# First attention with keys on partitions in a second score pass

## The reference

```
q = layernorm((x @ Wq.T) per head); k = layernorm((x @ Wk.T) per head); v = (x @ Wv.T) per head
scores = where(causal, q @ k.T, -1e30)
x = softmax(scores) @ v, heads joined, @ Wo.T + bo
```

## Time and profile before

| what | us |
|---|---|
| runs, lowest / median / highest | 4074.95 / 4082.11 / 4089.76 |
| profiled execution, its own time | 4099.86 |
| its span | 4098.0 |
| TensorE, VectorE, ScalarE busy | 3508.8, 3057.7, 2302.6 |
| GpSimd busy | 805.5 |
| probability transposes, TensorE busy | 730.8 |
| block copies on VectorE / ScalarE | 597.5 / 233.0 |
| accumulator reads on ScalarE | 437.6 |

### The profile page before, as it was taken

The page is one execution under the profiler, slowest core; times in us unless marked ns, Lnnn a source line. Parts: engine busy times, 40 slices in busy tenths (PEclk is TensorE's granted clock), DMA queues, the critical chain, the costliest instruction groups (busy, mean ns, idle before and its releaser), DMA issues.

```text
span 4098.0 us, 93072 instructions
## 1 busy us (share of the span) xinstructions
PE 3508.8 (86%) x31392; PEld 2764.5 (67%) x31392; DVE 3057.7 (75%) x6444; ACT 2302.6 (56%) x6346; POOL 805.5 (20%) x951
## 2 busy tenths in 40 slices
PE   3898888989889898897988989888898888989888
PEld 2676766767667676676766767667676766767667
DVE  3778777687777877778777687877878777787776
ACT  2655546565465654646646466554656546565464
POOL 1212222022220222202222122221212222022220
PEclk9899999999999998999989989999999999999999
DMA  3000000000000000000000000000000000000000
GB/s 73 7 2 7 7 7 7 2 7 7 7 7 2 7 7 7 7 1 12 2 7 7 7 7 2 7 7 7 7 2 7 7 7 7 2 7 7 6 2 6
DMA packets 33906, 30.35 MB, mean 7 GB/s; under 512 B 8864, under 2 KB 33312, under 8 KB 33376
## 3 DMA queue, kind: packets, MB, share of 16 engines
q1 hardware_dynamic: 33376, 23.68, 2.0%
HBM read 15.28 MB, written 8.39 MB: 6 GB/s over the span
## 4 chain that ended last, share of the span: by engine, by line
PE 57%; issue 14%; DVE 12%; ACT 10%; POOL 5%; SPq 1%; ACTq 0%; DVEq 0%; DMA 0%; POOLq 0%
PE bank L625 12%; PE scores L723 9%; ACT prob L839 6%; PE bank L636 6%; PE scores L612 6%; PE bank L735 4%; PE scores L613 4%; PE scores L614 3%; PE bank L596 2%; POOL qf L503 2%; PE scores L697 2%; PE scores L608 2%; PE scores L677 2%; DVE negmax L1055 1%; PE bank L555 1%
## 5 line engine op out<-in xcount | busy, mean ns | idle before, releaser
L839 ACT ACTIVATE prob<-scores,negmax 128x128 f32<-128x128 f32 (+3 forms) x2048 | 1060.7, 538 | 221.8 <-DVE negmax L1055 178.6
L1055 DVE TENSOR_REDUCE negmax<-scores 128x1 f32<-128x128 f32 (+3 forms) x2048 | 885.4, 484 | 101.0 <-PE scores L614 87.6
L625 PE MATMUL bank<-ident,prob 128*128 128x128 f32 x5120 | 730.8, 280 | 44.9 <-DVE probt L1063 35.6
L1063 DVE COPY probt<-bank 128x512 f32<-128x512 f32 x896 | 597.5, 685 | 179.2 <-PE bank L625 172.2
L625 PEld LDWEIGHTS bank<-ident,prob 128*128 128x128 f32 x5120 | 548.2, 142 | 156.0 <-DVE probt L1063 66.3
L614 PE MATMUL scores<-mask,ident 128*128 128x128 bf16 x2048 | 450.0, 231 | 0.0
L612 PE MATMUL scores<-khh,qt 128*128 128x256 f32 (+2 forms) x1024 | 438.4, 429 | 13.3 <-ACT qt L810 7.5
L839 ACT ACTIVATION_READ_ACCUMULATOR prob<-scores,negmax 128x1 f32 x2048 | 437.6, 214 | 0.0
L810 ACT ACTIVATE probt<-bank 128x512 f32<-128x512 f32 x384 | 233.0, 607 | 205.6 <-PE bank L625 205.6
L613 PE MATMUL scores<-kll,qt 128*128 128x256 f32 (+2 forms) x1024 | 345.4, 337 | 0.0
L596 PE MATMUL bank<-ident,stk 128*128 128x128 bf16 x2048 | 203.8, 286 | 153.2 <-DVE stk L1153 122.2
(11 more groups left out here) (179 smaller groups left out, 6967.4 us busy)
## 6 DMA issues: line engine op xcount, KB each, us to landing
x_in<-in_x_rows SPq DMA_DIRECT2D x16, 512.0 KB, 3.5
out_rows<-x SPq DMA_DIRECT2D x16, 512.0 KB, 3.6
r_gu<-in_wg SPq DMA_DIRECT2D x2, 512.0 KB, 5.0
r_gu<-in_wu SPq DMA_DIRECT2D x2, 512.0 KB, 5.5
r_d<-in_wd SPq DMA_DIRECT2D x1, 1024.0 KB, 6.8
r_wqt<-in_wq_nope_t SPq DMA_DIRECT2D x1, 512.0 KB, 6.2
r_wqr<-in_wq SPq DMA_DIRECT2D x2, 256.0 KB, 8.8
r_wob<-in_wo SPq DMA_DIRECT2D x1, 512.0 KB, 5.3
```

The costliest lines, as they stand in the source:

```text
L625: ins = nc.tensor.transpose(bank[4 + n % 2][:, q * P:(q + 1) * P], prob[:, u % 2, q, i * P:(i + 1) * P], ident[:, :])
L839: nc.scalar.activation(prob[:, u % 2, q, 0:n], bank[q][:, 0:n], ACT.Exp, bias=negmax[:, a, u, q:q + 1], accum_out=sums[:, a, u, q:q + 1]). ...
L1055: nc.vector.tensor_reduce(negmax[:, a, u, M * part:M * part + M], scores[:, M * part:M * part + M, 0:n], axis=AX.X, op=ALU.max, negate=Tru ...
L1063: nc.vector.tensor_copy(probt[:, u % 2, i], bank[4 + n % 2][:, :]).then_inc(probt_dve.sem, 1)
```

## The change

The second attention keeps its code (the index for which attention it is goes away). The first attention has an order of its own, `attend_first`:

- **First score pass.** `score_first` computes the scores with queries on partitions in 11 fills per group (`fill`: the four heads of tile 0 share a bank, two heads of tile 1 do, tiles 2 and 3 take a bank each), in a ring of banks 0 to 2. They are used only for the maximum (`max_first`).
- **The maximum as two rows.** VectorE splits a group's 16 columns of negated maxima in two bf16 parts (`split_max`), TensorE transposes them into bank 7, VectorE copies them to `nmt`, and SyncE moves them in two DMAs to partitions 96 and 97 of the query half of `qkt`, which is now 128 partitions deep. The padding of the keys is set to one, that of the queries to zero, so a product over 128 partitions gives score minus maximum.
- **Second score pass.** `score_keys` computes it with keys on partitions in 10 chunks of 512 columns per group, in a ring of banks 3 to 5, with the transposed mask. ScalarE's `exp_first` takes the exponential of a chunk with no bias and no sum, straight into `pt1`.
- **Values.** `weigh_first` multiplies `pt1` by `va` in one product per head and key tile (512, 384, 256 and 128 columns). Column 16 of `va` is one, so the sum comes out as a row.
- **Normalising.** The group's output is copied out, transposed to tokens on partitions, divided by its sum (`normalise_first`), gathered in `otok`, and after two groups transposed back as 128 full channels (`transpose_tok`), split by ScalarE and VectorE and projected with 24 matmuls (`project_first`).
- **Order.** While group g's chunks run, the fills of group g+1 stand between them (`FILL_AT`), the value products of group g-1 stand at chunks 2 and 3, and the maxima of g+1 are transposed after chunk 8. GpSimd has no part in it.
- **Setup.** The output weights load in one DMA, unpadded.

```diff
+FILLS = 11
+CHUNKS = 10
+S_RING, ST_RING, PAIRS = 3, 3, 3
+FILL_AT = ((0, 1), (2, 3), (4, 5), (6, 7), (8,), (9,), (10,), (), (), ())
+def fill(f):
+    if f == 0:
+        return 0, (0, 1, 2, 3)
+    if f < 3:
+        return 1, (2 * f - 2, 2 * f - 1)
+    return (2, (f - 3,)) if f < 7 else (3, (f - 7,))
...
+        def move_rows(b):
+            for g in range(NG):
+                sp.wait_ge(nmt_copied.sem, nmt_copied.at(b, g + 1))
+                for part in range(2):
+                    row = SD + part
+                    sp.dma_start(qkt[row:row + 1, g * G:(g + 1) * G, :].rearrange("o h (j q) -> o (h j) q", j=NT),
+                                 nmt[part * G * NT:(part + 1) * G * NT, g % 2]).then_inc(rows_moved.sem, 16)
...
-                nc.gpsimd.memset(stk[:, s, :, SPLITS:SLOTS], 0.0).then_inc(pad_ready.sem, 1)
+                nc.gpsimd.memset(stk[:, s, 0:H, SPLITS:SLOTS], 0.0).then_inc(pad_ready.sem, 1)
+                nc.gpsimd.memset(stk[:, s, H:2 * H, SPLITS:SLOTS], 1.0).then_inc(pad_ready.sem, 1)
...
+        def score_first(b, g, f):
+            j, heads = fill(f)
+            n = g * FILLS + f
+            keys = (j + 1) * P
+            out = bank[n % S_RING]
+            if n >= S_RING:
+                pe.wait_ge(max1_ready.sem, max1_ready.at(b, n - S_RING + 1))
+            for i, q in enumerate(heads):
+                h = g * G + q
+                mm(out[:, i * keys:(i + 1) * keys], qkt[0:SD, h, j * P:(j + 1) * P], qkt[0:SD, H + h, 0:keys], start=i == 0, stop=False)
...
+        def score_keys(b, g, c):
+            pair, kind = divmod(c, 5)
+            m = g * CHUNKS + c
+            out = bank[S_RING + m % ST_RING]
+            if c == 0:
+                pe.wait_ge(rows_moved.sem, rows_moved.at(b, 2 * 16 * (g + 1)))
+            if m >= ST_RING:
+                pe.wait_ge(exp1_ready.sem, exp1_ready.at(b, m - ST_RING + 1))
...
+        def weigh_first(b, g, i):
...
+            for q in range(G):
+                p = pt1[:, (2 * g + q // 2) % PAIRS]
+                e = q % 2
+                prob_ = (p[:, e, :], p[:, 2 + e, 0:3 * P], p[:, 4, e * 2 * P:(e + 1) * 2 * P], p[:, 2 + e, 3 * P:L])[i]
+                ins = mm(bank[6][q * HP:(q + 1) * HP, i * P:L], va[:, i, g * G + q], prob_, start=i == 0, stop=i == NT - 1)
...
+        def attend_first(b):
+            for f in range(FILLS):
+                score_first(b, 0, f)
+            transpose_max(b, 0)
+            for g in range(NG):
+                for c in range(CHUNKS):
+                    score_keys(b, g, c)
+                    if g + 1 < NG:
+                        for f in FILL_AT[c]:
+                            score_first(b, g + 1, f)
+                    if g > 0 and c in (2, 3):
+                        weigh_first(b, g - 1, 2 * c - 4)
+                        weigh_first(b, g - 1, 2 * c - 3)
+                    if g == 3 and c == 2:
+                        transpose_tok(b, 0)
+                    if g > 0 and c == 6:
+                        transpose_out(b, g - 1)
+                    if g + 1 < NG and c == 8:
+                        transpose_max(b, g + 1)
+            for i in range(NT):
+                weigh_first(b, NG - 1, i)
+            project_first(b, 0)
+            transpose_out(b, NG - 1)
+            transpose_tok(b, 1)
+            project_first(b, 1)
...
+        def attend_first(b):                 # ScalarE
+            for g in range(NG):
+                for c in range(CHUNKS):
+                    exp_first(b, g, c)
+                    if g > 0 and c == 4:
+                        copy_out_first(b, g - 1)
+                    if g == 3 and c == 2:
+                        split_first(b, 0)
...
+        def attend_first(b):                 # VectorE
+            for g in range(NG + 1):
+                if g < NG:
+                    for f in range(FILLS):
+                        max_first(b, g, f)
+                    split_max(b, g)
+                if g == NG:
+                    low_first(b, 0)
+                if g >= 2:
+                    normalise_first(b, g - 2)
+                if g < NG:
+                    copy_max(b, g)
+            normalise_first(b, NG - 1)
+            low_first(b, 1)
```

More of the change, by code:

```diff
@@ L416, in _ @@
         load(ebias[:, :], dram["ebias"].rearrange("(o d) -> o d", o=1).to_broadcast([P, E]))
[L418 to L421, removed]
+        load(r_woa[:, :, :], dram["wo1t"].rearrange("(k p) n -> p k n", p=P))
         sp.sem_inc(out_stored.sem, 16)
@@ L598, in transpose_stack @@
                 ins.then_inc(stackt_psum.sem, 1)
-        def score(b, a, u, part):
+        def score_first(b, g, f):
[8 more added lines that the diff above has]
+                mm(out[:, i * keys:(i + 1) * keys], qkt[0:SD, h, j * P:(j + 1) * P], qkt[0:SD, H + h, 0:keys], start=i == 0, stop=False)
+            r = len(heads)
+            diag = out[:, 0:r * keys].rearrange("p (r k) -> p r k", r=r)[:, :, keys - P:keys]
+            mm(diag, ident16[:, :], mask16[:, :].unsqueeze(1).to_broadcast([P, r, P]), start=False, stop=True).then_inc(s1_psum.sem, 1)
@@ L601, in score @@
+        def score(b, u, part):
             g, j = u // NT, tile_of(u)
             n = (j + 1) * P
+            m = max(n, 2 * P)
             for q in range(M * part, M * part + M):
@@ new lines, in transpose_tok, with project_first @@
+        def transpose_tok(b, k):
+            pe.wait_ge(otok_ready.sem, otok_ready.at(b, 2 * k + 2))
+            if k == 0:
+                pe.wait_ge(nmt_copied.sem, nmt_copied.at(b, NG))
+            for t in range(NT):
+                ins = nc.tensor.transpose(bank[7][:, t * P:(t + 1) * P], otok[:, t, k * P:(k + 1) * P], ident[:, :])
+            ins.then_inc(o1_psum.sem, 1)
+        def project_first(b, k):
+            for t in range(NT):
+                if t == 0:
+                    pe.wait_ge(o1h_ready.sem, o1h_ready.at(b, k + 1))
+                    pe.wait_ge(o1l_ready.sem, o1l_ready.at(b, k + 1))
+                for m, (x_, w_) in enumerate(TERMS):
+                    ins = mm(bank[t][:, 0:C], (o1h, o1l)[x_][:, k, t * P:(t + 1) * P], woa[:, w_, k],
+                             start=m == 0 and k == 0, stop=m == 2 and k == KC - 1)
+                if k == KC - 1:
+                    ins.then_inc(y_psum.sem, 1)
@@ L1050, in copy_q, with max_first @@
                                   bank[(4, 5, 7)[m % 3]].rearrange("p (h t) -> p h t", h=4)).then_inc(qt_dve.sem, 1)
-        def maxima(b, a, u, part):
+        def max_first(b, g, f):
+            j, heads = fill(f)
+            n = g * FILLS + f
+            r, keys = len(heads), (j + 1) * P
+            dve.wait_ge(s1_psum.sem, s1_psum.at(b, n + 1))
+            nc.vector.tensor_reduce(nm1[:, g, heads[0]:heads[0] + r, j], bank[n % S_RING][:, 0:r * keys].rearrange("p (r k) -> p r k", r=r),
+                                    axis=AX.X, op=ALU.max, negate=True).then_inc(max1_ready.sem, 1)
@@ L1079, in attend @@
                     for part in range(NM):
-                        maxima(b, a, u, part)
+                        maxima(b, u, part)
                 mine = []
```

338 lines of the change are left out of this document (220 added, 118 removed).

## The result

The kernel after takes 4324.40 us (median of 4 runs, 4312.52 to 4333.42) against 4082.30 for the kernel before (4 runs, 4074.95 to 4089.76): a ratio of 1.0591 [1.0555, 1.0627]. The forecast was 4250 with a range of 4040 to 4400, and slower with a chance of 0.75.

What follows compares the result with a forecast made beforehand. It took the first attention as bound by three nearly full engines handing to each other. +94 for the stage, +80 clock, -2 setup gave +172: 4272 from the profiled execution, 4254 from the median, forecast 4250, range 4040 to 4400.

Steps and rivals of the forecast that it cites:

- The sum at 2.4 GHz: First attention stage, one batch at full clock: 66.4 us against 60.5 before, +5.9 each, +94 over 16 batches.
- The handoff: From a group's last maximum to its second score pass: splits, transpose, copy, two transfers, wake-ups, 4.3 us, four exposed per batch.
- The row of the 8 KB table: Trace transfer used as stand-in for moving the maxima: landing 2.4 us, so the pair costs 2.9.
- The work: First attention, engine work per group: by work alone a group falls from 13.2 to about 9.5 us.
- rival D: Value product: wide f32 product costs 3.6 us a group, not 2.4; +50, inside the forecast's range, no separate chance.
- TensorE's idle stretches: Sign in the new stage: waits for rows_moved near 3.5 us, three per batch, and one near 7 at the first.
- the clock's term: First attention: half clock at the start of each phase after TensorE waits, +5 us a batch, +80 over 16.
- group 3 and the tail: End of the first attention stage: within the clock's term, the half clock costs 1 us there.
- Setup: Before the batches: one 256 KB weight load instead of four strided ones behind a memset, -2 us.
- Rival A: First attention: same path, but the fills keep TensorE at 2.4 GHz; 4174 us, chance 0.2.
- Rival B: First attention: short handoff, work decides, stage 55 us, 3990 us; faster 0.2, balance within 0.3% 0.05.
- Rival C: First attention: clock halved nearly throughout, or transfers at 4.6 us; each about 4400 to 4450, chance 0.08.

Runs made afterwards that it cites:

- experiment 3: Kernel after, with useless TensorE products ahead of each wait for the maxima's rows and of the first maxima transpose; 4201.73 us, ratio 1.0262 to the kernel before.
- experiment 1: Kernel after, with maxima moved to spare space, left out of the exponent, and TensorE not waiting for them; 4089.08 us, ratio 0.9983 to the kernel before.
- experiment 5: Kernel after, with fills a group further ahead, maxima transposed at chunk 4 and their copy ahead of the normalising; 4051.17 us, ratio 0.9875.
- experiment 6: Same as experiment 5, but both rows of the maxima go in one transfer instead of two; 4036.79 us, ratio 0.9849 to the kernel before.
- experiment 4: Kernel after, with all four value products at chunk 6 and output transposes one chunk later; 4326.03 us, ratio 1.0560 to the kernel before.
- experiment 9: As experiment 4, with maxima transposed between the value products, copied ahead of the normalising, and output transposes after chunk 8; 4176.15 us, ratio 1.0200.

## Why the prediction was right, point by point

The direction, the mechanism and the range held. The forecast was 74 us low, and one term was mis-sized for most of it.

**The sum at 2.4 GHz** was 66.4 us for a stage. Six of experiment 3's stages at a clock of 1.00 took 66.2. Within it, start and group 0 were shorter (batch 2 of experiment 3: 10.1 and 10.4 us, predicted 11.0 and 11.3), groups 1 and 2 were as predicted (13.35 each, 13.2), and from chunk 0 of group 3 to the end it took 19.0, not 17.7. That the sum met the stage is partly luck: 1.8 us too much ahead of group 1 stand against 1.3 too little at the end. The stage before was put at 60.5 us; by the same border it averages 60.7.

**The handoff** was put at 4.3 us. From the last maximum to chunk 0 it took 3.35 at the first two of a batch (mean of 16; in batch 3 from 915.63 to 0.4 us ahead of the mask at 919.34), and 4.4 and 4.1 at the other two, where the normalising stands ahead of the copy (predicted 4.75). The parts erred in both directions: two transfers start 0.55 apart, not 0.47, and land after 1.7 us, not 2.4; SyncE needed 0.03 behind the copy, not 0.2. From copy to chunk 0 it was 2.4 to 3.0, predicted 3.2. The row of the 8 KB table was too dear as a stand-in; the page "DMA: Bandwidth & Descriptors" of the Trainium skill, section "Anatomy of one DMA", gave about 2.0 us (its figure is for transfers issued by GpSimd, these are SyncE's) and came nearer, but the measured 1.7 is under it too, and the measurement decides.

**The work** came as predicted where it could be read: eleven maxima 6.14 us (6.1); a group's value products 2.36 at 2.4 GHz (the prediction's terms give 2.34 for one run and 2.48 with two, where it wrote 2.4), so rival D, 3.6 a group, is out; exponentials 0.48 to 0.49 apart where they follow one another (0.49), 0.60 each. TensorE's idle stretches, forecast near 3.5 us, three per batch, and near 7 in the first part, were 2.2 to 2.8 in batch 3, and 5.6 in that part (10.50 less 4.86 busy).

**The step that failed is the clock's term,** "+5, +80 over 16 batches". Its form was right, half a clock behind each wait, and its size was not. The stage averages 74.05 us and takes 66.17 where fillers hold the clock (with the issue of the load as its end): 7.9, not 5. The prediction gave group 3 and the tail 1 us together; the last part of batch 3 took 21.9 us (962.14 to 983.99) where experiment 3 needed 19.0, and the value products at its head took 3.22 us instead of 1.71. It put the clock behind the stage at nothing without a reason: the rest of a batch lost 1.6 us, at 0.88 instead of 0.90 (and 3.2 us at 0.87 in experiment 1, so the waits alone don't explain it). In the profiled execution these are 46 and 24 us more than forecast, the sum at 2.4 GHz 10 less (5.3 a batch, not 5.9), the start 2 less: 172+58 = 230, against 233.6 measured.

**Setup:** the first load was issued 2.25 us earlier, at 74.10 (predicted 2); the first stage started 3.9 earlier.

**Rival A** (clock stays up, 4174) did not happen, but its price was nearly right: with the fillers of experiment 3, whose stages took 66 to 68 us in ten batches of 15 and about 70 in five, 4201.73. **Rival B** (a handoff under 2.8 us, 3990) did not happen as put, the handoff being 3.4 to 4.4. Its core, that work decides once the handoff is covered, is what experiments 5 and 6 show, at 4051 and 4037: not 55 us a stage but 56 to 57. In batch 3 of experiment 5 the first exponentials of the groups come 11.1 us into the stage and then 7.8, 9.5 and 8.9 us apart, with 19.0 to the end; the rival had 9.0, three times 9.5, and 17.7 from chunk to chunk. The groups are shorter than it said, the bare start (ScalarE is busy 0.65 of the first 11.4 us) and the end longer. **Rival C** did not happen: the clock was never at the lower level throughout, and no transfer of this kind was near 4.6.

**What the prediction took as given** was the order of the work. It named the normalising ahead of the copy as 0.45 us; in experiment 4 this order cost 2.17 us of waiting and kept a better place of the value products from paying. How much of experiment 9's gain is this order alone isn't shown, since it moved the transposes too.

## What to carry to other kernels

An exchange like this one, over VectorE, TensorE, SyncE's transfer and back, took 3.0 to 4.4 us for 8 KB, on average, in one transfer or two; count how often it is bare before counting the work that it saves, and issue its inputs a whole group ahead (the same change lost 5.9% with 2.4 us bare in each group and won 1.2 to 1.5% with all but the start covered). Price TensorE's clock along with each such wait: here it cost 7.9 us a batch within the stage, beside 9.6 us of idle TensorE. Where a result is awaited elsewhere, its copy belongs ahead of anything in the same queue that can itself wait.

## What the runs showed of the hardware

- A DMA from 16 partitions to one, 4 KB inside SBUF, lands 1.7 us after its issue (median of 128, 1.6 to 2.4); two on one queue start 0.55 to 0.57 us apart. One of 8 KB lets TensorE start 2.0 us behind the copy's end, the pair 2.4 to 2.6 (means). No transfer of before was under 2.3.
- An f32 product of four heads side by side costs for each 128 columns the same at 512 columns as at 128: 512+384+256+128 columns of four heads, 32 records, took 2.36 us at 2.4 GHz, and 16 records (512 and 384) 1.71.
- In the kernel after, idle stretches of 2.2 to 2.9 us on TensorE, four in 74 us, went with a granted clock of 0.80 to 0.86 over the stage; the same stretches filled with useless products went with 1.00 in the best stages and 0.90 to 0.93 in five of 15, where the clock was 0.67 or 0.68 up to the first exponential. Why two stages of the same program with the same fillers differ stays open.
